# Two-layer transformer on one core: the second attention's score operands laid out by head on 32 partitions each

## The reference

```python
def _L1_attn_ref(x, w_qkv, w_proj, b_proj):
    H, D = 16, 8                                   # heads, channels of a head
    qkv = grouped_linear(x, w_qkv, None)           # 8 groups of 16 channels
    q, k, v = qkv[0] * D ** -0.5, qkv[1], qkv[2]
    attn = softmax(einsum('bhnd,bhmd->bhnm', q, k))
    out = einsum('bhnm,bhmd->bhnd', attn, v)
    return grouped_linear(out, w_proj, b_proj)
```

## Time and profile before

| | us |
|---|---|
| three runs | 982.16, 982.47, 984.56 (median 982.47) |
| the profiled execution's own time | 984.84 |
| its span, first to last instruction | 983.1 |
| busy: TensorE matmul / VectorE / ScalarE / GpSimd | 792.4 / 649.1 / 524.2 / 344.6 |
| mean granted TensorE clock | 0.934 |

### The profile page before, as it was taken

The page is one execution under the profiler, slowest core; times in us unless marked ns, Lnnn a source line. Parts: engine busy times, 40 slices in busy tenths (PEclk is TensorE's granted clock), DMA queues, the critical chain, the costliest instruction groups (busy, mean ns, idle before and its releaser), DMA issues. The chain is left out here.

```text
span 983.1 us, 12967 instructions
## 1 busy us (share of the span) xinstructions
PE 792.4 (81%) x4212; PEld 497.0 (51%) x4212; DVE 649.1 (66%) x1290; ACT 524.2 (53%) x970; POOL 344.6 (35%) x389
## 2 busy tenths in 40 slices
PE   3547888988898889999989899789989888527850
PEld 2233444555454667787767544345344444227740
DVE  3135568676663777776768696488898876347853
ACT  1013454545556677776757456456656656217740
POOL 3413775543532000000005345653453542133425
PEclk9987999999999999999999979899999999659985
DMA  4251331102110490000002112210110200011013
GB/s 125 48 95 21 85 81 35 34 22 46 30 24 2 137 285 6 1 1 1 1 8 57 43 42 63 60 35 17 38 25 18 58 4 10 4 54 56 32 34 84
DMA packets 56414, 44.75 MB, mean 46 GB/s; under 512 B 6598, under 2 KB 47387, under 8 KB 56347
## 3 DMA queue, kind: packets, MB, share of 16 engines
q1 hardware_dynamic: 55323, 41.82, 16.8%
q0 software_dynamic: 1024, 2.10, 0.7%
HBM read 14.67 MB, written 14.55 MB: 30 GB/s over the span
## 5 line engine op out<-in xcount | busy, mean ns | idle before, releaser
L926 ACT ACTIVATE ring<-single 128x512 f32<-128x512 f32 (+3 forms) x512 | 253.1, 517 | 226.3 <-PE single L1176 218.8
L1554 DVE TENSOR_REDUCE mneg<-pair 128x2 f32<-128x1024 f32 (+3 forms) x256 | 258.5, 1022 | 87.7 <-PE pair L1160 33.2
L1176 PE MATMUL single<-q_op,k_op 104*128 104x512 f32 (+3 forms) x512 | 216.5, 443 | 17.8 <-ACT ring L926 9.2
L1156 PE MATMUL pair<-k_op,q_op 96*128 96x512 f32 (+3 forms) x512 | 172.1, 415 | 42.2 <-DVE mneg L1554 22.6
L786 POOL TENSOR_SCALAR k_op<-k_stk,cst 104x512 fp32r<-104x512 f32 x64 | 100.0, 1577 | 276.2 <-DMA k_stk<-hl 258.5
L1176 PEld LDWEIGHTS single<-q_op,k_op 122*128 122x128 f32 (+1 forms) x512 | 97.9, 197 | 98.6 <-ACT ring L926 72.6
L1156 PEld LDWEIGHTS pair<-k_op,q_op 120*128 120x128 f32 (+1 forms) x512 | 98.9, 207 | 86.8 <-DVE mneg L1554 44.8
L1192 PE MATMUL p_o<-ring,vaug 128*9 128x512 f32 (+3 forms) x1024 | 116.1, 526 | 1.0 <-ACT ring L926 0.9
L721 POOL TENSOR_SCALAR_AFFINE_SELECT ring<-ring 128x256 f32<-128x256 f32 x128 | 52.3, 408 | 149.4 <-ACT ring L926 149.2
L955 ACT ACTIVATE ring<-pair,cols 128x512 f32<-128x512 f32 x136 | 86.1, 685 | 33.8 <-PE pair L1236 27.5
L1600 DVE TENSOR_TENSOR ring<-ring,single 128x1024 f32<-128x1024 f32 x60 | 73.3, 1221 | 45.5 <-ACT ring L955 44.4
(11 more groups left out here) (294 smaller groups left out, 1306.4 us busy)
## 6 DMA issues: line engine op xcount, KB each, us to landing
xs<-zero SPq DMA_DIRECT2D x10, 1024.0 KB, 10.1
q_op<-hl SPq DMA_DIRECT2D x96, 64.0 KB, 2.0
stage<-in_L_ffn_W_dram SPq DMA_DIRECT2D x8, 512.0 KB, 4.5
stage<-in_L_ffn_rW_dram SPq DMA_DIRECT2D x6, 512.0 KB, 5.1
k_op<-hl SPq DMA_DIRECT2D x48, 64.0 KB
k_stk<-hl SPq DMA_DIRECT2D x48, 64.0 KB, 2.0
xb<-xs SPq DMA_DIRECT2D x15, 128.0 KB, 2.0
xs<-yb SPq DMA_DIRECT2D x15, 128.0 KB, 1.7
```

What stands on the lines that cost most here:

```text
L926: exp_done.by(act.activation(ring[:, n % 8, lo:T], singles[n % 2][:, lo:T], ACT.Exp), (L, n))
L1156: ins = pe.matmul(both[:, i, 0:hi], r32(qs[:, P * qt:P * (qt + 1)]), r32(ks[:, 0:hi]), start=i == 0 or L == 1 or qt >= 2, stop=L == 1)
L1176: st_full.by(pe.matmul(singles[n % 2][:, lo:T], r32(ks[:, P * kc:P * (kc + 1)]), r32(qs[:, lo:T]), start=True, stop=True), (L, n))
L1554: s_taken.by(dve.tensor_reduce(mneg[:, G % 2, 2 * p:2 * p + 2, qt], both[:, :, 0:hi], axis=AX.X, op=ALU.max, negate=True), (L, m))
```

## The change

Each head of a group gets 32 partitions of its own in both operands. Within them, channel d has four rows, 4d to 4d + 3: for q they are high, high, low, and 0; for k they are high, low, high, and a row that is 1 for channels 0 and 1 and 0 for the others. The rows 3 and 7 of q's 32 later take the two parts of the maxima. To get this layout with one transfer per operand, ScalarE and VectorE write the terms into four planes each of a new buffer `hl1`; ScalarE's rounded copy now writes two planes in one instruction (1024 columns in place of 512). GpSimd sets planes 3 and 7 once. The masks, `k_op1` and `k_masked` are gone: a group's maxima wait for the transfers themselves. The matmuls contract 32 rows; TensorE's operands are the partitions 32j to 32j + 31 for head j. The number of matmuls, their columns, the order of all parts and the first layer stay as they are.

```diff
@@ constants
-    for j in range(GH):
-        c[:, C_HM + j] = ((p < 96) & (p % GH == j)) | (p == 96 + j) | (p == 96 + GH + j)
+    c[:, C_HM] = p % HD < 2
@@ buffers
-        k_op1 = put("k_op1", [P, 4 * GH, T], at=at_op)
+        hl1 = put("hl1", [P, 8, T], at=at_op + 16 * KB)
...
-        M_ROWS, H_ROWS, R_ROWS = 32, 16 * 6, 16 * 6
+        M_ROWS, H_ROWS, H_ROWS1, R_ROWS = 32, 16 * 6, 16 * 2, 16 * 6
...
+        HIGH1, LOW1 = {"q": slice(0, 2), "k": slice(4, 7, 2)}, {"q": 2, "k": 5}
@@ head1_dma
                 for w, part in enumerate(("q", "k")):
                     taken.wait_ge(sp, (part, NB + r))
-                    for t in range(3):
-                        sp.dma_start((q_op1, k_stk)[w][32 * t:32 * (t + 1), g, :],
-                                     hl[32 * g:32 * g + 32, 2 * w + TERM[w][t], :]).then_inc(head_rows1[g], 16)
+                    sp.dma_start((q_op1, k_stk)[w][:, g, :], hl1[32 * g:32 * g + 32, 4 * w:4 * w + 4, :]).then_inc(head_rows1[g], 16)
@@ m_dma
-                        dst = q_op1[96 + GH * part:96 + GH * (part + 1), G % NG, :]
+                        dst = q_op1[3 + 4 * part:P:32, G % NG, :]
@@ second_weights
-                pool.tensor_scalar(by_dim(w_q[1][:, :]), by_head(w_qkv[:, 0:D]), SCALE1, None, ALU.mult)
-                pool.tensor_copy(by_dim(w_k1[:, :]), by_head(w_qkv[:, D:2 * D]))
+                pool.tensor_scalar(w_q[1][:, :], w_qkv[:, 0:D], SCALE1, None, ALU.mult)
+                pool.tensor_copy(w_k1[:, :], w_qkv[:, D:2 * D])
@@ gpsimd, before the layer
-            pool.memset(k_stk[96:P, :, :], 1.0).then_inc(k_ones, 1)
+            steps.step(pool.memset(hl1[:, 3, :], 0.0))
+            pool.tensor_scalar(hl1[:, 7, :], hl1[:, 3, :], cst[:, C_HM:C_HM + 1], None, ALU.add).then_inc(k_ones, 1)
@@ gpsimd, the layer: mask() is removed, and with it its calls
-            for G in range(3):
-                mask(G)
             for s in range(NB, STAGES):
-                G = NG * (s - NB)
                 add_bias(s)
-                mask(G + 3)
...
@@ scalar, part q or k
-                            act.wait_ge(head_rows1[g], H_ROWS * (s - NB))
+                            act.wait_ge(head_rows1[g], H_ROWS1 * (s - NB))
...
-                    hi_ready.by(act.activation(r32(hl[:, 2 * w, :]), src[:, :], ACT.Copy), key)
+                    if L:
+                        hi_ready.by(act.activation(r32(hl1[:, HIGH1[name], :]), src[:, :].unsqueeze(1).broadcast_to([P, 2, T]), ACT.Copy), key)
+                    else:
+                        hi_ready.by(act.activation(r32(hl[:, 2 * w, :]), src[:, :], ACT.Copy), key)
@@ tensor, operands
-                rows_in = 96 if K == 24 else 104
-                return q_op1[0:rows_in, G % NG, :], k_op1[0:rows_in, GH * ((G + 2) % 4) + j, :]
+                return q_op1[32 * j:32 * j + 32, G % NG, :], k_stk[32 * j:32 * j + 32, G % NG, :]
@@ tensor, max_unit
-                        k_masked.wait_ge(pe, G)
+                        pe.wait_ge(head_rows1[G % NG], H_ROWS1 * (G // NG + 1))
@@ vector, part q or k
-                    take(key, dve.tensor_tensor(r32(hl[:, n + 1, :]), src[:, :], hl[:, n, :], ALU.subtract))
+                    hi, lo = (hl1[:, 2 * n, :], hl1[:, LOW1[name], :]) if L else (hl[:, n, :], hl[:, n + 1, :])
+                    take(key, dve.tensor_tensor(r32(lo), src[:, :], hi, ALU.subtract))
```

More of the change, by code:

```diff
@@ L40 @@
 NBLK = T * NB // 256 + E1 - 1
-C_N = C_HM + GH
+C_N = C_HM + 1
 B_MS, B_TRI, B_ONE = 0, P, 2 * P
@@ L402, in build @@
         head_rows1 = [sem(f"head_rows1_{g}") for g in range(NG)]
-        k_masked = sig("k_masked", list(range(4 * NG)))
         rope_rows = sem("rope_rows")
@@ L800, in _ @@
                     modulate(s - 1)
-                if s < STAGES - 1:
-                    mask(G + 4)
                 if s == NB:
@@ L805, in _ @@
                         weights1(n)
-                if s < STAGES - 1:
-                    mask(G + 5)
                 if s == NB:
@@ L812, in _ @@
                     scatter(s - 1)
-                if s < STAGES - 1:
-                    mask(G + 6)
             modulate(STAGES - 1)
```

## The result

The changed kernel takes 1004.49 us (median of 4 runs, 994.52 to 1018.29); the kernel before took 982.32 beside it (979.23 to 984.56). The ratio is 1.0194, with an interval of 1.0108 to 1.028; it leaves out the execution of 1018.29, which lies over 1.5% above the fastest. The forecast of 963 us and its range are wrong. What came is the rival with a chance of 0.1, "the clock falls", whose time was 1004.

What follows compares the result with a forecast made beforehand. TensorE's order, VectorE's work and late masks were taken as close limits. Terms -22 (masks), -6 (overlap), +5 (shape changes), +3 (copy) gave -20 us, 963 us against the 982.5 median; own range 955 to 972, with side rivals 948 to 978.

Steps and rivals of the forecast that it cites:

- the clock falls: Rival, chance 0.1: quarter-row matmuls running two at a time bring half level; 21 steps x 2.0 us, net +22, 1004 us.
- What bounds the kernel: Second attention: TensorE's order and VectorE's work lie close together as limits, with late masks on top.
- the 60, 64, 64 and 58 us: Expected lengths of the second attention's stages 0 to 3 in the next profile, each given as near.
- The masks: GpSimd's masks gone: 15 us of waits, 4 of half-level clock, 3 of stretched VectorE instructions; 22 us less.
- Changes of shape: TensorE switching between 32-row scores and other parts: 63 changes at 0.1 to 0.2 us, half on the path, +5 us.
- The overlap: A unit's two 32-row maxima matmuls run side by side on TensorE; 6 us less.
- row groups overlap with everything: Rival, chance 0.12: neighbouring heads' scores and units also overlap, changes of shape cost nothing; -32 us, 950.
- ScalarE's copy: Copy of q and k widened from 512 to 1024 columns delays later parts: 6 x 0.46, 3 us more.
- The landing: The 256 KB operand transfer inside SBUF was taken to land in 2.7 us, from a transfer out of HBM.
- the cover of 7 us: Operand transfers have more than two steps, 7 us, before use; nothing would wait even if landing took double.
- granted clock near 1.00 in all four: Expected in the next profile: TensorE's granted clock near 1.00 in all four stages of the second attention.
- The signs of being wrong: Maxima waiting for transfers, stages 1 and 2 staying above 67 us, or the clock in them under 0.9.

Runs made afterwards that it cites:

- experiment 2: The changed kernel with every score matmul contracting all 128 rows of the stack, so heads are summed and the answer is wrong: 962.35 us, ratio 0.9782.
- experiment 3: The changed kernel with each head's k rows among zeros, so 128 rows are contracted and the answer is right, five transfers a group: 961.78 us, ratio 0.9773.
- experiment 8: experiment 2's kernel with four added matmuls a step: of 32 rows 1180.61 us; as control, of 128 rows, 997.39 us.
- experiment 4: experiment 3's kernel with 32 rows for the maxima alone, 977.75 us; for the scores alone, 1056.96; 64 rows for both, 978.44.
- Experiment 5: experiment 3's kernel with ScalarE's rounded copy of q and k back at 512 columns: 961.69 us, ratio 0.9809.

## Why the prediction was wrong

**What bounds the kernel** (three limits close together) was right. In experiments 2 and 3, with the masks gone and the clock kept, the four stages came out within 1 us of the 60, 64, 64 and 58 us that the prediction named. That these two kernels also took 962.35 and 961.78 us, next to its 963, is partly luck: only the terms of the masks and the copy apply to them.

**The masks**, -22: right, -21.9 in the layer of experiment 2. Their three parts weren't separated, but VectorE's stretch was seen to go (345 to 163 ns), and the clock of 0.93 in stage 0 to rise to 1.00.

**Changes of shape**, +5 at 0.1 to 0.2 us each: the size of one was right (0.17 by experiment 8, 0.09 by experiment 4's stage, 0.1 to 0.2 by its timeline). The count of 63 leaves out those at the values, which change rows as well now: in the change the values start 0.43 us after the last score (723.70 to 724.13), where it was 0.33. That changes may also cost clock is not in the prediction. The Trainium skill ("TensorEngine Tiling (Array Packing)", Key Properties) says that a change of tiling mode drains the engine. The traces now agree for rows, with the 0.17 us a change of experiment 8.

**The overlap**, -6: it happens, and goes further than assumed, between scores and maxima too. Where the change kept full level it is worth more than forecast. Here are steps 48 to 52 and 53 to 63 of the layer, first in the change, then in experiment 3's kernel (windows from first exponential to first exponential):

```profile
785.20:802.90 17.70, 14.21 (x97) 5.71 (x97) 14.36 (x28) 12.22 (x24) 0.00 (x0) 1.00 0.28 56
802.90:857.80 54.90, 48.70 (x189) 16.35 (x189) 24.44 (x79) 26.34 (x51) 6.45 (x6) 0.51 0.02 6
```

```profile
761.40:780.70 19.30, 18.21 (x99) 9.09 (x97) 15.31 (x28) 12.94 (x26) 0.00 (x0) 1.00 0.23 51
780.70:818.90 38.20, 34.15 (x190) 14.54 (x189) 23.46 (x79) 26.44 (x51) 6.43 (x6) 1.00 0.03 9
```

At full level in both, five steps take 17.70 against 19.30 us, 0.3 us less a step, with the changes of shape paid. In stage 2, where VectorE is the limit, the first twelve steps, again at full level in both, take 47.7 against 48.5 us, 0.06 less a step. If the 32 steps of stages 0 and 3 and the 32 of stages 1 and 2 all ran so, the change would be 12 us under 962, which is the rival "row groups overlap with everything" (950): an estimate, since no run held the level.

**ScalarE's copy**, +3: too much. Experiment 5 shows no cost in the whole time and 0.9 us in the layer. The prediction added its 0.46 us to the path for all six; most of it was covered. **The landing** of 256 KB, 2.7 us: wrong, 3.8 and 4.5, and harmless, as the cover of 7 us said: no weight load of the maxima waits for a transfer.

**The step that failed** is the last line of what the next profile would show, "granted clock near 1.00 in all four", and under it the chance of 0.1 for the clock. The reasons against that rival were the earlier trace rows: at matmul busy 13.05 of 16 us the clock had been 1.00. That row is from matmuls of 104 rows. It says nothing of matmuls of 32, and the change altered exactly that; what the runs showed in its place is 0.59 and 0.63 in stages 0 and 3, and 1.00 again once all rows are named (experiment 2). The signs of being wrong were set on stages 1 and 2. They came, though barely (stage 1 has 67.50 us for the 67 and 0.89 for the 0.9), while nearly all of the loss is in the other two. The rival's mechanism was right in its first half (a quarter of the rows) and wrong in its second (two at a time): with the overlap the clock was higher, not lower. Its size was right by two errors that cancel. It reckoned 21 steps at half level and 2.0 us for each. In the change some 28 of 64 steps were there (a mean of 0.75 means that half of the 284.3 us were at half level, and a step there takes about 5.0), and one costs 1.5 us against the full-row kernel in the windows above: (54.90 - 38.20) / 11. Steps 9 to 16, at half level too, give much the same: 41.8 us against 28.5, 1.7 a step. The account, an estimate from these windows, closes: 267.5, less 21.9 for the masks, is 245.6. 28 steps of 1.5 us are 42 more, and the steps at full level give back some 3 (1.6 and 0.8 us in the two stretches above, 17 of the 36 steps). That makes 285; the layer took 284.3.

## What to carry to other kernels

Before splitting a matmul into row groups, ask what the granted clock stands on: a kernel whose TensorE works near its limit can lose more to the half level than it gains from the overlap. Where a head needs only 32 rows, contracting all 128 with zeros in the rest took the same stream time (0.46 us for a pair of maxima, as the 0.47 of 32 rows without overlap), needed no change between 32 and 128 rows and kept the clock at 1.00; the kernel built so is 2.3% faster than the kernel before, by the masks that it saves. When a profile row is used as a witness that something won't happen, look first whether the row has the property that the change alters.

## What was not expected of the hardware

- 128 added matmuls over all rows cost the change nothing: 996.56 and 994.62 us with them, 1004.49 and 1001.78 without. Half as many cost time: 1018.78 us with 64.
- 256 added full-row matmuls in the full-row kernel (experiment 8's control) cost 35 us, 962.35 to 997.39, or 0.14 us each. The same number with 32 rows cost 172 and 265 us.
- Executions of one kernel differ by up to 93 us (1134.2 and 1227.02, experiment 8 with 32 rows; 1013.02 to 1091.47, scores alone on 32 rows), the longer ones at the lower clock. The full-row kernels of experiments 2, 3 and 5 stayed within 5 us each.
- A transfer of 256 KB inside SBUF, 32 partitions of 8 KB into 128 partitions of 2 KB, lands after 3.8 to 4.5 us, where 64 KB took 2.0.
